# Two-layer transformer on one core: where the output bias is added, how many row buffers the last stage has, when slots are read, and which engine multiplies in the last norm

## What is computed

```python
x = _layernorm(x + _L0_attn_ref(x, ...))          # causal attention, 16 heads of 128, rope, latent keys and values
x = _layernorm(x + _L0_ffn_ref(x, ...))           # SwiGLU of 688 with low-rank experts chosen per token
x = _layernorm(x + _L1_attn_ref(x, ..., Wo, bo))  # linear attention: relu(q) (sum relu(k) v) / (q . sum k), then @ Wo + bo
x = _layernorm(x + _L1_ffn_ref(x, ...))           # 64 experts of 176, top 6, capacity 32 rows each, plus a shared SwiGLU of 352
```

## Time and profile before

| | |
|---|---|
| runs timed | 1520.21, 1521.79, 1521.89 us; median 1521.79 |
| the profiled execution | 1516.38 us, its span 1513.6 us |
| mean granted clock of PE | 0.973 of 2.4 GHz |
| busy share | PE 93%, PE weight loads 74%, DVE 62%, ACT 38%, POOL 37% |
| chain that ended last, by engine | PE 80%, DVE 8%, POOL 4%, issue 3%, DMA 2%, ACT 2% |

### The profile page before, as it was taken

The page is one execution under the profiler, slowest core; times in us unless marked ns, Lnnn a source line. Parts: engine busy times, 40 slices in busy tenths (PEclk is TensorE's granted clock), DMA queues, the critical chain, the costliest instruction groups (busy, mean ns, idle before and its releaser), DMA issues.

```text
span 1513.6 us, 23841 instructions
## 1 busy us (share of the span) xinstructions
PE 1405.4 (93%) x8106; PEld 1120.8 (74%) x8106; DVE 940.7 (62%) x2170; ACT 569.8 (38%) x1441; POOL 554.1 (37%) x483
## 2 busy tenths in 40 slices
PE   7999999999999999899999799999999999768980
PEld 6777777777777777677777588788788788655650
DVE  4677777777777777764343565665665656656114
ACT  4444444444444444532222233333333333322320
POOL 3555555555555555201014123522531512204223
PEclk9999999999999999999999899999999999879985
DMA  5000000000002000110000200200200003936984
GB/s 177 1 11 1 12 0 10 0 10 0 10 0 71 1 0 1 21 63 1 1 0 1 70 8 15 71 8 15 70 7 14 7 15 93 274 126 196 275 236 125
DMA packets 68220, 76.37 MB, mean 50 GB/s; under 512 B 14205, under 2 KB 55445, under 8 KB 68149
## 3 DMA queue, kind: packets, MB, share of 16 engines
q1 hardware_dynamic: 56789, 58.49, 13.6%
q10 hardware_dynamic: 8288, 12.22, 2.6%
q0 software_dynamic: 3072, 4.72, 1.6%
HBM read 66.22 MB, written 9.21 MB: 50 GB/s over the span
## 4 chain that ended last, share of the span: by engine, by line
PE 80%; DVE 8%; POOL 4%; issue 3%; DMA 2%; ACT 2%; SPq 0%; POOLq 0%; ACTq 0%; DVEq 0%
PE ps L1645 37%; PE ps L1772 9%; PE ps L1746 7%; PE ps L1734 5%; PE ps L1806 4%; PE ps L1897 4%; PE ps L1739 2%; PE ps L1980 2%; PE ps L2176 1%; PE ps L2111 1%; PE ps L1970 1%; DMA sums_dram<-rows 1%; PE ps L2193 1%; PE ps L1774 1%; PE ps L1736 1%
## 5 line engine op out<-in xcount | busy, mean ns | idle before, releaser
L775 ACT ACTIVATE probs<-ps,nm 128x128 f32<-128x128 f32 (+3 forms) x256 | 134.0, 526 | 151.1 <-DVE nm L1143 151.1
L629 POOL TENSOR_TENSOR qk<-q,ksb 128x512 f32<-128x512 f32 x64 | 82.6, 1291 | 293.5 <-ACT q L870 221.9
L1772 PE MATMUL ps<-kT,qT 128*128 128x128 f32 (+3 forms) x512 | 174.6, 450 | 5.2 <-ACT probs L775 4.5
L1067 DVE TENSOR_TENSOR pT_low<-ps,pT 128x384 fp32r<-128x384 f32 (+2 forms) x256 | 99.6, 451 | 123.1 <-ACT pT L711 121.9
L1084 DVE TENSOR_TENSOR prod<-ps,rope_sb 128x1024 f32<-128x1024 f32 x128 | 150.2, 1215 | 6.3 <-PE ps L1645 6.3
L507 POOL TENSOR_TENSOR qT<-prod 64x512 f32<-64x512 f32 x64 | 81.2, 1269 | 169.9 <-DVE prod L1084 131.4
L711 ACT ACTIVATE pT<-ps 128x384 fp32r<-128x384 f32 (+2 forms) x256 | 84.8, 416 | 152.4 <-PE ps L1806 152.4
L1746 PE MATMUL ps<-U,oT 128*128 (+1 forms) x512 | 124.5, 386 | 0.0
L507 POOL TENSOR_TENSOR kT<-prod 64x512 f32<-64x512 f32 x64 | 81.4, 1272 | 111.1 <-DVE prod L1084 108.7
L1143 DVE TENSOR_REDUCE nm<-ps 128x1 f32<-128x128 f32 (+3 forms) x256 | 113.7, 484 | 12.9 <-PE ps L1774 12.9
L1200 DVE SCALAR_TENSOR_TENSOR acc<-ps,rinv,acc 128x256 f32<-128x256 f32 x256 | 109.4, 479 | 11.9 <-PE ps L1746 11.9
(11 more groups left out here) (260 smaller groups left out, 2772.0 us busy)
## 6 DMA issues: line engine op xcount, KB each, us to landing
eg<-in_L_ffn_w_gate_dram SPq DMA_DIRECT2D x16, 704.0 KB
eg<-in_L_ffn_w_up_dram SPq DMA_DIRECT2D x16, 704.0 KB
ed<-in_L_ffn_w_down_dram ACTq DMA_DIRECT2D x10, 640.0 KB
ksb<-ks_dram SPq DMA_DIRECT2D x16, 256.0 KB, 3.3
ed<-in_L_ffn_w_down_dram SPq DMA_DIRECT2D x6, 640.0 KB
rows_dram<-rows ACTq DMA_DIRECT2D x4, 640.0 KB, 3.3
acc<-in_L_attn_x_dram SPq DMA_DIRECT2D x4, 512.0 KB
wq_in<-in_L_attn_wq_dram SPq DMA_DIRECT2D x8, 256.0 KB, 2.9
```

Source lines behind the costliest of these rows:

```text
L629: nc.gpsimd.tensor_tensor(qk[:], q3[:], ksb[b % 2][:], ALU.mult).then_inc(qk_ready, 1)
L775: nc.scalar.activation(probs[hh][:, off:off + (i + 1) * P], ps[:, BS + i % 2, 0:(i + 1) * P], ACT.Exp, bias=nm[:, hh, i:i + 1], accum_out= ...
L1067: return nc.vector.tensor_tensor(o, whole, hi.bitcast(F32), ALU.subtract)
L1772: pe.matmul(ps[:, bank, 0:(i + 1) * P], qT[:, hh, b, i * P:(i + 1) * P], kT[:, hh, b, 0:(i + 1) * P], start=True, stop=False)
```

## The change

It does four things.

1. The four bias instructions become `add_bias(b)`. Batches 0, 1 and 2 are done inside `ffn0`'s last batch, batch 3 in the second step of the block of batch 1 of chunk 0.
2. `rows` has a third buffer (at 85 KB), and each batch's stores count on a semaphore of their own (three reuse old ones). `store_rows` waits for no store, `rows4` only for batch 3. The third buffer lies where the weights of expert group 5 go, so SP waits for batch 2's stores before it loads them.
3. `take_slots()` stands right behind `merge_lists()`, ahead of two `hidden4`.
4. DVE's `last_norm(b)` makes only `shift16 = -mean * rstd` (one instruction of 128x4), and ACT does `fin * rstd + shift`, four instructions a batch.

```diff
-        rows = [place(f"rows{i}", 56 + 5 * i, [P, TPB, ROW]) for i in range(2)]
+        rows = [place(f"rows{i}", at, [P, TPB, ROW]) for i, at in enumerate((56, 61, 85))]
+        rows_stored = [sem("rows_stored"), rope_loaded, la_loaded, dn_loaded]
+        rows_stored_first = (0, 16, 16 * 8, 16 * 13)
+        def wait_rows(engine, b):
+
+            engine.wait_ge(rows_stored[b], rows_stored_first[b] + (48 if b == 0 else 32))
@@ -465,6 +472,7 @@
             sp.wait_ge(sw_lo, 2)
+            wait_rows(sp, 2)
             load_experts(5)
@@ -688,7 +696,8 @@
             pool.wait_ge(idx_ready, 2)
-            pool.wait_ge(rows_stored, 32 * BATCH + 16)
+            for b in range(BATCH):
+                wait_rows(pool, b)
@@ -961,15 +970,13 @@
             def store_rows(b):
                 act.wait_ge(scored, b + 1)
-                if b:
-                    act.wait_ge(rows_stored, 32 * b + 16)
-                here = rows[b % 2]
+                here = rows[b % 3]
@@ -1058,6 +1065,12 @@
             outputs4(GROUPS - 1)
+
+            for b in range(BATCH):
+                act.wait_ge(shift_ready, b + 1)
+                for t in range(b * TPB, b * TPB + TPB):
+                    nc.scalar.activation(fin[:, t, :], fin[:, t, :], ACT.Identity, bias=shift16[:, t:t + 1],
+                                         scale=rstd16[:, t:t + 1]).then_inc(out_done, 1)
@@ -1278,6 +1291,11 @@
+            def add_bias(b):
+                dve.wait_ge(x2lo_ready, b + 1)
+                r = acc[:, b * TPB:(b + 1) * TPB, :]
+                return nc.vector.tensor_tensor(r, r, bo_sb[:].rearrange("p (a n) -> p a n", a=1).broadcast_to([P, TPB, D]), ALU.add)
+
@@ -1292,13 +1310,18 @@
                     if m == 3 and last:
                         x2_rests(0, 4)
+                    if m == 4 and last:
+                        dve.wait_ge(dn_loaded, 13 * 16)
+                        link(add_bias(0))
                 if not last:
                     route0(b + 1)
                 else:
                     x2_rests(1, 4)
+                    link(add_bias(1))
                 for i in range(TPB):
                     if last and i == 2:
                         x2_rests(2, 4)
+                        link(add_bias(2))
@@ -1403,6 +1426,9 @@
                         if i < 3 and not (last and b == 3):
                             keys(n + 1, i + 1)
+                        if first and b == 1 and i == 1:
+                            link(add_bias(3))
+                            settle()
@@ -1410,12 +1436,6 @@
             x2_rests(3, 4)
 
-            dve.wait_ge(dn_loaded, 13 * 16)
-            dve.wait_ge(x2lo_ready, BATCH)
-            for b in range(BATCH):
-                r = acc[:, b * TPB:(b + 1) * TPB, :]
-                link(nc.vector.tensor_tensor(r, r, bo_sb[:].rearrange("p (a n) -> p a n", a=1).broadcast_to([P, TPB, D]), ALU.add))
-            settle()
             dve.wait_ge(zeroed, 5)
@@ -1441,12 +1461,12 @@
                 dve.wait_ge(rstd_ready, b + 9)
-                if b >= 2:
-
-                    dve.wait_ge(rows_stored, 32 * (b - 1) + 16)
+                if b >= 3:
+
+                    wait_rows(dve, b - 3)
@@ -1537,9 +1557,9 @@
             merge_lists()
+            take_slots()
             hidden4(1, 1)
             hidden4(1, 2)
-            take_slots()
@@ -1626,9 +1646,9 @@
                 dve.wait_ge(rstd_ready, 13 + b)
-                for t in range(b * TPB, b * TPB + TPB):
-                    nc.vector.tensor_scalar(fin[:, t, :], fin[:, t, :], meanvar16[:, t, 0:1], rstd16[:, t:t + 1],
-                                            ALU.subtract, ALU.mult).then_inc(out_done, 1)
+                at = slice(b * TPB, b * TPB + TPB)
+                nc.vector.scalar_tensor_tensor(out=shift16[:, at], in0=meanvar16[:, at, 0], scalar=-1.0, in1=rstd16[:, at],
+                                               op0=ALU.mult, op1=ALU.mult).then_inc(shift_ready, 1)
```

More of the change, by code:

```diff
@@ L85, in program @@
         ebias = place("ebias", 17.5, [P, E0])
-        scratch = place("scratch", 17.75, [P, 1])
+        scratch = place("scratch", 17.875, [P, 1])
         xT = [place(f"xT{h}", 20 + 16 * h, [P, KD, TOK], F32R) for h in range(2)]
@@ L202, in program @@
         rstd16 = place("rstd16", 17.125, [P, TILES])
+        shift16 = place("shift16", 17.75, [P, TILES])
         xg = place("xg", 56, [P, GROUPS, ROW])
@@ L272, in program @@
         out_done = sem("out_done")
+        shift_ready = sem("shift_ready")
         wq3_loaded, wk3_loaded, wv3_loaded, wo3_loaded = (
@@ L963, in store_rows @@
                 act.wait_ge(scored, b + 1)
[L964 to L967 removed]
+                here = rows[b % 3]
+                nc.scalar.dma_start(rows_dram[b * T:(b + 1) * T, :].rearrange("(i p) n -> p i n", p=P), here[:]).then_inc(rows_stored[b], 16)
                 nc.scalar.dma_start(sums_dram[b * T:(b + 1) * T, :].rearrange("(i p) n -> p i n", p=P),
[L969 removed]
+                                    here[:, :, 0:D]).then_inc(rows_stored[b], 16)
                 if b == 0:
                     nc.scalar.dma_start(sums_dram[TOK:TOK + 2 * P, :].rearrange("(i p) n -> p i n", p=P),
[L972 removed]
+                                        here[:, 0:2, 0:D]).then_inc(rows_stored[b], 16)
             def gate4(b, m):
@@ L1443, in rows4 @@
                 dve.wait_ge(rstd_ready, b + 9)
-                if b >= 2:
-                    dve.wait_ge(rows_stored, 32 * (b - 1) + 16)
+                if b >= 3:
+                    wait_rows(dve, b - 3)
                 for i in range(TPB):
                     t = b * TPB + i
-                    nc.vector.tensor_scalar(rows[b % 2][:, i, 0:D], acc[:, t, :], meanvar16[:, t, 0:1], rstd16[:, t:t + 1],
+                    nc.vector.tensor_scalar(rows[b % 3][:, i, 0:D], acc[:, t, :], meanvar16[:, t, 0:1], rstd16[:, t:t + 1],
                                             ALU.subtract, ALU.mult).then_inc(x3_ready, 1)
@@ L1495, in choose @@
                 link(nc.vector.memset(top4[:, :, TOP1:8], -1.0))
-                nc.vector.tensor_tensor(rows[b % 2][:, :, D:ROW], e4[:], bcast(sm4[:].rearrange("p (i a) -> p i a", a=1), [P, TPB, E1]),
+                nc.vector.tensor_tensor(rows[b % 3][:, :, D:ROW], e4[:], bcast(sm4[:].rearrange("p (i a) -> p i a", a=1), [P, TPB, E1]),
                                         ALU.mult).then_inc(scored, 1)
@@ L2063, in turn_x3 @@
                     for i in range(TPB):
-                        last = pe.transpose(ps[:, k, i * P:(i + 1) * P], rows[b % 2][:, i, k * P:(k + 1) * P], ident[:])
+                        last = pe.transpose(ps[:, k, i * P:(i + 1) * P], rows[b % 3][:, i, k * P:(k + 1) * P], ident[:])
                     last.then_inc(x3_turned, 1)
```

6 lines of the change are left out of this document (1 added, 5 removed).

## The result

| | before | after |
|---|---|---|
| runs timed together | 1521.84 us median (1520.21 to 1522.40, 4 runs) | 1501.68 us median (1499.67 to 1503.93, 4 runs) |
| ratio, 95% interval | | 0.988 [0.9865, 0.9895] |
| the profiled execution, its span | 1516.38, 1513.6 | 1501.84, 1499.3 |
| mean granted clock of PE | 0.973 | 0.974 |

The forecast was 1501.6 us, 20.2 us less than before; 20.2 us came out. It is not as clean as it looks: the two profiled executions lie only 14.5 us apart, so a loss that I had not forecast is in the second, and the experiments found a gain that I had not forecast.

What follows compares the result with a forecast made beforehand. PE was taken as the bound, busy for 93% of the span, with gains in its waits. Terms 8.8 + 9.9 + 0.4 + 1.1 = 20.2 us took 1521.8 to 1501.6 us, ratio 0.987; range 1496 to 1508.5.

Steps and rivals of the forecast that it cites:

- Bias, 8.8 us: Start of the linear attention: moving four bias instructions wins 9.2 us and gives back 0.4; ends 6.3 and 9.5 us.
- I take the long duration, 2.2 us: Batch 3's bias addition, beside POOL's `qk`, takes 2.2 us on DVE, giving back 0.4 us on PE's path.
- Third row buffer, 9.9 us: Last stage: `rows4(2)` stops waiting for stores; 8.4 us of wait and 1.5 of clock won; ends 7 and 11 us.
- the cover: Last stage: `rows4(3)` needs batch 0's stores at 1334.6; without group 5's weights they were expected at about 1324.
- The new wait of SP: Group 5's load waits for batch 2's stores, issued about 1341 and landed 1345.5; claimed to cost nothing in the last stage.
- Slots, 0.4 us: Before the first gathered rows: gather starts 1.5 us earlier, but only 0.4 us is won; ends 0 and 1.5.
- The expert ring keeps its length: Expert stage: groups 6 to 15 move with PE; the 3.25 us wait and slow stretch behind it were left as they were.
- the clock, 4%, 5 us: Rival, 4%: the expert ring loses its one slow stretch, winning 5 us more, for 1497 us.
- Last norm, 1.1 us: Tail: ACT does the multiplications, four taking 1.9 us, and ends at 1509.0 against 1510.16; ends: gain 1.9, loss 0.7.
- The median of the runs is 5.4 us above it; I keep that distance: Whole kernel: profiled execution goes from 1516.4 to 1496.2 us, with the median of the runs still 5.4 us above it.
- signs for "wrong": `rows4(3)` waiting for a DMA, an expert group over 4 us, POOL for rows, or ACT over 0.7 us per multiplication.
- the trace shows the clock down only behind idle times of over 3 us: PE's clock: slow only behind waits of 7.25, 9.12, 3.33 and 3.25 us, so full clock was counted after shorter ones.

Runs made afterwards that it cites:

- the first group: Four runs (kernel before and full change repeated, bias alone, third row buffer alone) measured beside the kernel before, whose median there was 1515.74 us.
- The third group: Four runs (both large parts, outputs scaled before down weights are issued, full change, row buffer alone) measured beside the kernel before, whose median there was 1520.74 us.
- the full change, again: The changed kernel, unchanged, run for a second trace against the kernel before: 1493.65 us, ratio 0.9858, 22.1 us less.

## Why the prediction was right, and where it wasn't

- **Bias, 8.8 us: right.** 8.3 measured alone, 9.14 in the trace. PE resumed at 859.60 (forecast 859.65) and the transposes came at 863.90 (863.84). The step that failed is small: "I take the long duration, 2.2 us" for the fourth addition. It took 1.22 us. It was POOL's `qk` beside it that was lengthened, 2.13 instead of 1.29 us. PE lost nothing: from these transposes to those of the step after the last addition's it is 84.46 us (863.90 to 948.36), before 84.47 (873.04 to 957.51). The 0.4 us taken back were not there.
- **Third row buffer, 9.9 us: right.** 9.9 and 10.5 us alone. Wait and slow stretch went as said. In the trace 9.0 us are won at the marks (1337.99 to 1319.87, less the 9.14 of the bias) and not 9.9, since `rows4(2)` came 1.1 us later than counted; 1.1 us more are won in the down products behind it (4.38 against 5.49 us), which the prediction had left as they were. Batch 0's last store was to land in under 10 us and took 13.0 us (issued at 1307.12, so landed at 1320.1). `rows4(3)` began at 1326.38; the cover was 6.3 us and not 10. Without group 5 in the queue the store was only 2 us faster than the 15 us of the earlier trace rows: I had thought that group 5's weights were what held it, and they were not. The new wait of SP cost nothing in the last stage, as forecast.
- **Slots, 0.4 us: right in its sense.** The gather goes out 1.02 us behind the start of `turn_slots`, before 2.54 us. Of this 1.5 us, 1.0 are lost again before the first reload; the slots alone give 1.0 us less, the full change without them 0.9 us more than with them, both within the intervals.
- **"The expert ring keeps its length": wrong.** Without a stall it is 2 to 3 us shorter with both large parts in (the table), which is about what 22.1 has above 18.2 + 0.4 + 1.1. I had this as a rival (the clock, 4%, 5 us). What I left out is that the change can move the landings of the weights in the ring: the twelfth group's came up to 11 us earlier, and the wait of 3.25 us that I had left as it was the earlier trace rows went to under 1 us. Why they came earlier is open. "It moves with PE" was right at the first reload and wrong as a statement on the length: the stream takes its 82 us, and PE ends with it or, behind a late wait, some 3 us after it.
- **Last norm, 1.1 us: right**, 1.03 us (18.16 to 17.13). Batch 3's variance came 2.4 us earlier relative to the first addition (12.82 against 15.25 us). Four multiplications on ACT took 2.08 us, not 1.9. "ScalarE: Activation LUTs" of the Trainium skill, section "Rules for kernel authors", would keep multiplications and additions on VectorE. For one instruction the trace agrees (1.38 us for four on DVE, 2.08 on ACT), but the DVE queue in front decided. The estimate from that page's cost, 2.06 us, was nearer than my row (the copy of `y_in`). Giving only the last batch back to DVE took a further 1.65 us off, and the last store, which landed later, gave 1.1 back.
- **"The median of the runs is 5.4 us above it; I keep that distance": it did not hold, and the forecast came out by luck.** The profiled execution of the change lay at its median (1501.84 against 1501.68). By my sum it should have come out at 1496.2. That 20.2 us came out to a tenth all the same is luck: the same change gave 22.1 us in the first group and 18.0 us in the third. Its stall cost some 12 us between gather and reload and the ring behind it was 4 to 5 us shorter than in the two profiles of before (104.6 against 108.8 and 109.7 us). The third group, where the kernel before is at 1520.7 and all four profiles have a stall, and the first two, where it is at 1515.6 and none of eight has one, suggest that before has something of the kind in its slower measurements. No profile of before was taken in the third group, so this isn't shown; the one profile beside such slower measurements, the first of before (1516.38 us against 1520.21 to 1522.40 us), has no stall, which fits.
- Of the signs for "wrong", none of the rival mechanisms came: `rows4(3)` waited for no DMA, POOL for no rows, ACT took 0.59 us for each multiplication, no expert group waited over 4 us for its weights. The waits over 4 us that did come, PE's of 4.49 and 5.86 us in the stall, have another place and form than any that I named.
- **"the trace shows the clock down only behind idle times of over 3 us": misread.** The trace of before has one more slow stretch, behind an idle time of 2.79 us:

```profile
1298.39 1.66 PE L2064 MATMUL ps<-ident,rows 128*128 128x128 f32 x8 [2.79 <-DVE rows L1449]
```

  From 1298.7 to 1302.1 the granted clock is 0.50. No term of the sum changes by it, since the idle times that the prediction priced at full clock were of about 1 us.

## What to carry to other kernels

Count a removed wait together with the slow stretch behind it: both large terms came from an idle time and its stretch at 1.2 GHz, and measured within 0.6 us of the sum. Where a full stream of transfers sets a stage's end, ask where in the stage the engine waits: early waits and slow stretches cost nothing that showed here, and a late one some 3 us. And keep the profiled execution apart from the median: a gap of 5 us between them was a sign of something that the profile didn't show, and I should have asked what.

## Unexpected from the hardware

- When DVE's 128x1024 addition and POOL's 128x512 multiplication overlap, it isn't always DVE that is slowed: in the earlier trace rows the addition took 2.20 instead of 1.21 us and POOL kept its 1.27; here the addition took 1.22 and POOL 2.13. In the first case POOL began 0.16 us earlier, in the second DVE began 0.25 us earlier. Both times the one that began later was slowed.
- The clock doesn't go by the length of one idle time alone. In the full change, again, it fell behind one of 1.80 us; in the kernel without early slots it stayed up behind one of 2.34 us.
- PE's signal came 9 to 10.4 us late, in one piece or two, while POOL issued its gathers. This is in five profiles, the first of the changed kernel and the four of the third group, and in none of the nine others, two of them of the kernel before.
- With the third row buffer the gathers land later, and ACT's first two issues of down weights block for longer. Without it the median time from issue to landing of the gathers is 2.9 to 3.1 us and the two issues take 0.8 us (five profiles); with it they are 3.8 to 4.5 and 2.9 to 3.4 us (four profiles without a stall). No run tried why.
